# Score groups interleaved with value products in attention, and a quantiser whose transposes are issued one tile later

## What is computed

```python
def bitlinear(x, W, b):
    w_scale = jnp.clip(jnp.mean(jnp.abs(W)), EPS, None)
    Wq = _ste(W, jnp.clip(jnp.round(W / w_scale), -1.0, 1.0) * w_scale)
    x_scale = jnp.clip(jnp.max(jnp.abs(x), axis=-1, keepdims=True), EPS, None)
    xq = _ste(x, jnp.clip(jnp.round(x * (QB / x_scale)), -QB - 1.0, QB) * (x_scale / QB))
    return jnp.einsum('bnd,hd->bnh', xq, Wq) + b
...
q, k, v = (proj(Wq), proj(Wk), proj(Wv))
attn = jax.nn.softmax(jnp.einsum('bhqd,bhkd->bhqk', q, k) * SCALE, axis=-1)
out = jnp.einsum('bhqk,bhkd->bhqd', attn, v)
...
x = x + attention(xn) + bitlinear(gelu(bitlinear(xn, W1, b1)), W2, b2)
```

## Time and profile before

| | |
|---|---|
| median of the runs | 11071.7 us (11024.9 and 11118.5) |
| profiled execution | 11095.7 us, span of its slowest core 11094.7 us |
| spans of the cores | 10966.5 to 11008.9 us on die 0, 11058.7 to 11094.7 us on die 1 |
| mean granted TensorE clock | 0.76 on die 0, 0.73 to 0.75 on die 1 |
| busy, core 6 | PE 52%, DVE 28%, ACT 21%, POOL 1% |
| attention core of layer 1 | 5782 to 6812 us, 8584 to 9586 us |
| feed-forward net of layer 1, from the first product | 7055 to 8307 us, 9829 to 11095 us |

### The profile page before, as it was taken

One profiled execution on the slowest core, in us unless ns is written; L12 is line 12 of the kernel. 1 busy time (PEld: TensorE's weight loads), 2 busy tenths in 40 slices (PEclk: granted clock), 3 DMA queues, 4 the chain that ended last, 5 costly groups with the idle time before them and its releaser, 6 DMA issues.

```text
span 11094.7 us, 92223 instructions; the slowest of 8 cores (10966.5 to 11094.7 us)
## 1 busy us (share of the span) xinstructions
PE 5763.6 (52%) x33686; PEld 3472.2 (31%) x33686; DVE 3077.8 (28%) x4361; ACT 2320.9 (21%) x2412; POOL 131.9 (1%) x197
## 2 busy tenths in 40 slices
PE   0111124455785454468668884255445888425544
PEld 0010012232453232235435553122222555312222
DVE  3423422222101222210122124522233222452223
ACT  0000010000112100011115552211221555321212
POOL 1000000000000000000000000000000000000000
PEclk9999996666796666678867676677677777667776
DMA  7463511221232212223200000022110000002221
GB/s 185 146 137 118 153 60 61 68 69 62 87 121 82 74 61 69 68 78 115 89 23 5 5 5 8 28 79 80 67 61 25 5 5 5 8 27 80 80 68 61
DMA packets 366364, 728.17 MB, mean 66 GB/s; under 512 B 126438, under 2 KB 126695, under 8 KB 361832
## 3 DMA queue, kind: packets, MB, share of 16 engines
q1 hardware_dynamic: 310088, 525.13, 14.8%
q0 software_dynamic: 55840, 197.15, 6.1%
HBM read 663.48 MB, written 77.59 MB: 67 GB/s over the span
## 4 chain that ended last, share of the span: by engine, by line
PE 42%; DMA 21%; DVE 18%; ACT 9%; issue 6%; ACTq 2%; DVEq 1%; SPq 1%; POOLq 0%; POOL 0%
PE pot L1696 7%; PE p1h L1332 4%; PE ph L1033 4%; PE pss L1654 4%; ACT c1At L1658 4%; DMA wna<-L_ffn_W 3%; PE pob L1062 3%; PE pq L778 3%; DMA wnb<-L_ffn_W 3%; PE p1o L1448 3%; DMA f1wf<-s_w2t 2%; PE pk L820 2%; PE pk L822 2%; DMA gwall<-s_L_attn_WqB 1%; DMA gwall<-s_L_attn_WvB 1%
## 5 line engine op out<-in xcount | busy, mean ns | idle before, releaser
L1658 ACT ACTIVATE c1At<-pss,shift_col 128x1024 bf16<-128x1024 f32 x1024 | 1077.0, 1112 | 688.7 <-PE pss L1654 685.0
L1654 PE MATMUL pss<-c1qch,a1kfm 64*128 64x256 bf16 x4096 | 701.9, 311 | 324.7 <-ACT c1At L1658 309.7
L1696 PE MATMUL pot<-c1At,a1vtok 128*65 128x256 bf16 x4096 | 825.7, 387 | 0.0
L1696 PEld LDWEIGHTS pot<-c1At,a1vtok 128*65 128x65 bf16 x4096 | 636.7, 162 | 180.8 <-issue 80.9
L1392 PE MATMUL p1u<-ident_bf,f1q2s 128*128 128x128 bf16 x1024 | 129.6, 302 | 942.5 <-ACT f1q2s L1379 918.5
L1332 PE MATMUL p1h<-xqfm,f1wf 128*128 128x512 bf16 x2048 | 499.1, 389 | 117.3 <-DMA f1wf<-s_w1t 112.1
L1654 PEld LDWEIGHTS pss<-c1qch,a1kfm 64*128 64x128 bf16 x4096 | 370.4, 103 | 583.6 <-issue 495.0
L820 PE MATMUL pk<-gwall,xnfm 128*128 128x512 bf16 x768 | 354.0, 461 | 361.3 <-DMA gwall<-s_L_attn_WvB 172.9
L1033 PE MATMUL ph<-xnfm,f0w 128*128 128x512 bf16 x2048 | 511.9, 415 | 48.7 <-DMA f0w<-s_w1t 35.1
L1062 PE MATMUL pob<-f0stash,f0w 128*128 128x256 bf16 x4096 | 494.3, 286 | 40.0 <-DMA f0w<-s_w2t 29.4
L1448 PE MATMUL p1o<-f1wf,f1ght 128*128 128x512 bf16 x2048 | 473.7, 388 | 47.9 <-DMA f1wf<-s_w2t 37.4
(11 more groups left out here) (217 smaller groups left out, 7455.2 us busy)
## 6 DMA issues: line engine op xcount, KB each, us to landing
wna<-L_ffn_W SPq DMA_DIRECT2D x128, 512.0 KB, 5.3
wnb<-L_ffn_W SPq DMA_DIRECT2D x32, 2048.0 KB, 12.1
f0w<-s_w1t SPq DMA_DIRECT2D x128, 512.0 KB, 3.6
f0w<-s_w2t SPq DMA_DIRECT2D x128, 512.0 KB, 3.7
f1wf<-s_w1t SPq DMA_DIRECT2D x128, 512.0 KB, 3.6
f1wf<-s_w2t SPq DMA_DIRECT2D x128, 512.0 KB, 3.7
gwall<-s_L_attn_WqB POOLq DMA_DIRECT2D x16, 2048.0 KB, 9.7
gwall<-s_L_attn_WkB POOLq DMA_DIRECT2D x16, 2048.0 KB, 9.7
```

Of the source, the lines that this page charges most:

```text
L1654: mm = b.pe.matmul(psp[k][:, kt4 * QCH:(kt4 + 1) * QCH], kf, qf, start=True, stop=True)
L1658: se_done[k] = b.tick(b.se.activation(Ath[:, kg * 4 * QCH:(kg + 1) * 4 * QCH], psp[k][:], AF.Exp, bias=st.shift_col[:], scale=0.125), "se")
L1696: mm = b.pe.matmul(potp[h % 2][:], va, Ath[:, kt * QCH:(kt + 1) * QCH], start=(kt == 0), stop=(kt == NKT - 1))
```

## The change

In the attention core, `emit_scores(h)` becomes `emit_scores_grp(h, kg)`, which emits one of the four groups. The first head's groups are emitted together as before. In the loop, groups 0 and 1 of head h+1 come ahead of the value products of head h, group 2 comes behind the eighth of the 16, and group 3 behind the sixteenth, ahead of `emit_ot` of head h-1. In the feed-forward net, the body of the quantiser is cut into three functions: `emit_red` (reductions and small steps), `emit_sr` (scaling and rounding) and `emit_trq` (transposes and copies back). Tile t runs `emit_red(t)`, then `emit_trq(t-1)`, then `emit_sr(t)`; the transposes of the last tile follow behind the loop. The statistics have two tiles in turn, and ACT waits for a given count of PE, that of the transposes of the tile before (for the first tile those of the block before), where it waited for PE's whole count.

```diff
-    qst = A("qst", [P, 4], F32)
+    qst2 = [A(f"qst{i}", [P, 4], F32) for i in (0, 1)]
...
-        for tt in range(4):
+        def emit_red(tt):
             gt_sl = ght[:, tt * FF:(tt + 1) * FF]
+            qst = qst2[tt % 2]
             b.ve.drain()
             b.wait(b.ve, "se")
             b.ve.reduce_max(qst[:, 0:1], gt_sl[:, 0:2048], axis=AX.X,
...
             b.tick(b.ve.drain(), "ve")
+
+        def emit_sr(tt, tr_gate):
+            gt_sl = ght[:, tt * FF:(tt + 1) * FF]
+            qst = qst2[tt % 2]
+            qv = 0
             for hh in range(2):
                 hsl = slice(hh * 2048, (hh + 1) * 2048)
                 b.wait(b.se, "ve")
-                b.wait(b.se, "pe")
+                if tr_gate:
+                    b.se.wait_ge(b.sem["pe"], tr_gate)
...
+            return qv
+
+        def emit_trq(tt, qv):
             with (nc.psum_tensor(_psname(st, "p1u"), [P, 512], BF16) as pu0,
                   nc.psum_tensor(_psname(st, "p1u"), [P, 512], BF16) as pu1):
                 pup = [pu0, pu1]
                 b.wait(b.pe, "se", qv)
...
+            return pv
+
+        qpend = None
+        for tt in range(4):
+            emit_red(tt)
+            if qpend is not None:
+                tr_gate = emit_trq(*qpend)
+            else:
+                tr_gate = prev_trq
+            qv = emit_sr(tt, tr_gate)
+            qpend = (tt, qv)
+        prev_trq = emit_trq(*qpend)
...
-            def emit_scores(h):
+            def emit_scores_grp(h, kg):
...
-            emit_scores(0)
+            NG = NKT // 4
+            for kg in range(NG):
+                emit_scores_grp(0, kg)
             pend = None
             for h in range(H):
                 if h + 1 < H:
-                    emit_scores(h + 1)
+                    for kg in range(min(2, NG)):
+                        emit_scores_grp(h + 1, kg)
                 b.pe.wait_ge(b.sem["se"], exps_of[h])
...
                     mm = b.pe.matmul(potp[h % 2][:], va,
                                      Ath[:, kt * QCH:(kt + 1) * QCH],
                                      start=(kt == 0), stop=(kt == NKT - 1))
+                    if kt == 7 and h + 1 < H and NG > 2:
+                        emit_scores_grp(h + 1, 2)
                 pv = b.tick(mm, "pe")
+                if h + 1 < H and NG > 3:
+                    emit_scores_grp(h + 1, 3)
                 if pend is not None:
                     emit_ot(*pend)
                 pend = (h, pv)
```

More of the change, by code:

```diff
@@ L1285, in _ffn1 @@
     prevo = {}
+    prev_trq = 0
     for ob in range(S // 512):
@@ L1378, in _ffn1 @@
                 b.wait(b.se, "ve")
-                qv = b.tick(b.se.activation(q2s[:, hsl], scf[:], AF.Identity,
+                qv = b.tick(b.se.activation(q2s[:, hh * 2048:(hh + 1) * 2048],
+                                            scf[:], AF.Identity,
                                             scale=qst[:, 2:3]), "se")
+            return qv
+        def emit_trq(tt, qv):
             with (nc.psum_tensor(_psname(st, "p1u"), [P, 512], BF16) as pu0,
@@ L1385, in _ffn1 @@
                 ev = {}
+                pv = 0
                 for jb in range(FT_ // 4):
@@ L1645, in emit_scores @@
                 Ath = At2[h % 2]
[L1646 to L1660, removed]
+                k = kg % 2
+                if k in se_done:
+                    b.pe.wait_ge(b.sem["se"], se_done[k])
+                for kt4 in range(4):
+                    kt = kg * 4 + kt4
+                    kf = kfm[(h % 2) * 64:(h % 2) * 64 + 64,
+                             (h // 2) * S + kt * P:(h // 2) * S + (kt + 1) * P]
+                    mm = b.pe.matmul(psp[k][:, kt4 * QCH:(kt4 + 1) * QCH],
+                                     kf, qf, start=True, stop=True)
+                pv = b.tick(mm, "pe")
+                b.wait(b.se, "pe", pv)
+                se_done[k] = b.tick(b.se.activation(
+                    Ath[:, kg * 4 * QCH:(kg + 1) * 4 * QCH], psp[k][:],
+                    AF.Exp, bias=st.shift_col[:], scale=0.125), "se")
                 exps_of[h] = se_done[k]
```

## The result

| | before | after |
|---|---|---|
| median | 11056.99 us (10 runs, 10947.62 to 11118.49) | 10734.1 us (11 runs, 10509.87 to 10886.75) |
| ratio, after to before | | 0.9592 [0.9494, 0.969] |
| profiled execution, span | 11094.7 us | 10552.6 us |
| granted TensorE clock over the span, by core | 0.732 to 0.764 | 0.787 to 0.802 |

A forecast was written before the change was run, and what follows sets the result against it. Bound: an attention chain alternating between PE and ACT, whose gaps also lower PE's clock. From the profiled 11095.7 us, less 406 (attention) and 20 (quantiser), 10670; median forecast 10645 us, range 10520 to 10780.

The forecast's parts named there:

- The head: Attention loop, one head: 7.25 us in the old trace; forecast 4.85 at 2.4 GHz, 5.58 at 0.81, 5.14 on the mean.
- The term for changes between score and value products: PE in the attention loop: four switches between the product kinds a head at 0.07 us, 0.28 together.
- the share of the middle level: Attention on the slowest cores: 40% of heads taken at granted clock 0.81, bounds none and all.
- The chunk: Attention, 256 queries with 16 heads: 98.7 us against 124.1, so 406 us less over 16 chunks.
- The first head behind the thin start: Start of each attention chunk, where score groups still wait for one another: one head at the lower clock, 7.8 us.
- The gap: From the last head's first value product to the next chunk's: 21.2 us less two exponentials, 19.2.
- The quantiser: Second feed-forward layer: only first transposes go under the reduction; 11.7 us between tiles becomes 10.85, 20 us less in all.
- rival (2): Attention: granted clock at the middle level everywhere, heads 5.58 us, chunk 104.3, kernel 10735 us; chance 0.20.
- (1): The forecast itself, 10645 us; 10580 with no heads at clock 0.81, 10680 with six in ten; chance 0.60.
- (3): Attention: the clock swing survives, half of each head at 0.50, heads 6.3 us, kernel 10885 us; chance 0.10.
- (4): Attention gains nothing: PE's product changes stall it some 2 us a head; only the quantiser's gain remains, 11050 us; chance 0.06.
- (5): Slower: one gap a head holds the clock at 1.2 GHz through the chunk, 141.1 us, kernel 11325 us; chance 0.04.

The follow-up runs named there:

- e3: Kernel before, old order, with eleven unread score products a head placed in PE's two gaps: 10711 us median against 11063.75.
- e9: Kernel before, old order, with eleven unread value products a head ahead of the 16, on the path that sets the head: 11131.9 us median against 11036.9.
- e12: Kernel before, old order, with four unread score products a head in PE's gaps (3 and 1): 10932.6 us in one run, against 11036.87.
- e11: Changed kernel with group 2's four score products split into two pairs, behind the sixth and tenth value product: 11097.7 us; kernel before 11036.87.
- e5: Kernel before with only the attention half of the change, quantiser as before: 10777.7 us (four runs) against 11001.9.
- e6: Kernel before with only the quantiser half of the change, attention as before: 11074.9 us (one run) against 11001.9.
- e7: Changed kernel with quantiser waits naming the needed counts, and copies and reductions placed on DVE while ACT works: 10364.2 us, ratio 0.9353 to before.
- e10: Changed kernel with twelve of the 16 value products a head left out, so the output is wrong: 10670.7 us (three runs); kernel before 11036.87.

## Why the prediction was right, and where its sizes were off

**What bounds the kernel: right.** A chain that alternates between PE and ACT, with the clock following its gaps. e3, e9 and e12 show the second half, in which the argument was thinnest: with the gaps filled and the order left alone the clock is at 1.00 in the steady heads (0.94 over the attention) and the value products take half the time.

**The head: right in form, two terms off.** The chain is the one written down: from group 3's first product to group 1's it is 1.96 us in the trace as in the sum (6005.61 to 6007.57). The profile shows 0.65 us of them as idle where the prediction, which counted from starts, had near 1. The term for changes between score and value products was 0.07 each; it measured 0.11 (6003.08 to 6004.08 is eight products, 0.87, and 0.13; from there to 6004.62 four, 0.44, and 0.10; e11's two extra changes cost 0.22). So the head at the upper level is 5.01 us, not 4.85; just over the upper bound of 5.0. The other way went the share of the middle level, 40% of heads: in the profiled execution the cores' attention shows 1.00 and 0.50 alone. Together 5.01 us where 5.14 was forecast: two errors of opposite sign, so part of the nearness is luck. The Trainium skill ("TensorE: Matmul & The Clock Gate", Part 1, the warning on the peak-current limiter) would have had every head at 13/16; 195 of the 240 intervals between core 5's heads at 5.01 us and a window at 1.00 don't agree for this execution. Nor is the level held over the stage in e5's, where core 2 has 0.81 over 5950 to 5969 us and 1.00 over 6070 to 6110.

**The chunk: right.** Forecast 98.7 us, measured 96.5. The first head behind the thin start was put at 7.8 and took 6.75 to 7.98; in four chunks it was three or four heads and not one. The last head was 4.5 and took 4.6. The gap was 19.2 and took 17.8 to 18.2 but for two of near 19.5, as in PE's timeline of after:

```profile
5766.49 1.91 PE L1723 MATMUL pot<-c1At,a1vtok 128*65 128x256 bf16 x16 [1.29 <-ACT c1At L1682]
...
5770.36 7.15 PE L1642 MATMUL pq<-xnfm,a1wall 128*128 128x256 bf16 x64 [0.58 <-DVE c1otok L1704]
...
5784.28 1.07 PE L1723 MATMUL pot<-c1At,a1vtok 128*65 128x256 bf16 x4
```

Its 64 projection products take 7.15 us where the earlier trace rows had 7.88: the granted clock is 1.00 over them, where a window over those of the earlier trace rows reads 0.89. The prediction took the gap's products at their old price.

**The quantiser: right.** 11.7 us between ACT's last activation of a tile and its next one should become 10.85: it is 11.0 (7118.79 to 7129.79), and the row names the copy L1410 as what it waits for, as the prediction read from the waits. 0.74 x 24 = 18 us against 20. e6 shows it alone, e7 what the wait and the places together cost.

**The sum.** Forecast for the profiled execution 10670 us, measured 10553.6, 116 less. Attention gave some 440 and not 406; the quantiser's 18 of 20 are lost in FF stages that were 11 us longer on the slowest core; and 115 us, as much as the whole miss, lie ahead of layer 1's attention, where no line changed. There core 6 of before was granted 0.81 for 1038 us of the first 5600 and core 5 of after for none. This is scatter that the sum has no term for. The median, 10734 for a forecast of 10645, lies in the range, but 181 us over the profiled execution where the prediction allowed 50 either way for the scatter; its terms don't contain that. That the median lies 89 us from the forecast is therefore in part luck: its errors go both ways. That it nearly equals rival (2)'s 10735 proves nothing: the heads of 5.58 us are not in the trace of after.

**The rivals.** (1) is what happened. (2) and (3): not in the attention of the profiled execution of after, but both in e5's, which has the same attention. On its core 2, 21 heads take 5.64 us at 0.81, where (2) had 5.58; 67 take 6.88, swinging as (3) has it, but between 0.81 and 0.50, where (3) had 6.3. No rival joined the two, and by e5 the dearer one is the more frequent there. Only one execution of after has a trace, so how often such heads come in it is open. (4), a stall of some 2 us at changes of product: 4 x 0.11 = 0.44. (5), slower because one gap a head holds the clock at 1.2 GHz, was given 0.04, on the ground that the clock rose after a stretch at 0.50 in which PE was shown busy throughout. That ground was weak. In e11 PE is shown busy 78.31 of 80 us at 0.50 and nothing rises; 8.23 us a head there and 5.42 in e10 are this rival. The Trainium skill ("Trainium Kernel Development and Optimization", Performance Expectations) calls the matmul busy time a bad metric for how close a kernel is to roofline, because matmuls are pipelined. e11 agrees that it says little here: PE is shown busy 97.9% of the window at 0.50, where 32 products at 0.214 us make 6.85 of a head's 8.23, and 89% of a window at 0.91. Forecasting faster was right, but with two changes of product more a head the whole gain is gone (e11), and no row that the prediction shows tells the two apart. That the clock stayed up in after was in part luck.

## What to carry to other kernels

When PE shares a loop with another engine and the trace shows its products at two durations, price the loop at both clocks, and try unread products in the gaps first: that takes one small edit and says how much of the loop is the clock's (here four fifths of 201 us a sequence). Taking work or gaps out of such a loop isn't safe by count alone: e11 was slower than after with equal work, and e10's attention with less. A reordering that leaves a wait on an engine's whole count gets little (18 us here); naming the counts that are needed, with the work placed in the gaps that this opens, gave 286.

## What the runs showed of the hardware

- Unread products made the kernel faster: eleven a head in PE's gaps, 10711 us against 11064.
- Leaving out three quarters of the value products made the attention slower, 814 to 824 us a sequence against 792 to 803, with nearly every head at a granted clock of 0.50 (e10).
- The same loop has steady heads of 5.01 us at a granted clock of 1.00; where the upper level is 0.81 it takes 5.64, or swings between 0.81 and 0.50 at 6.88 (e5, core 2).
- The same instructions have two steady paces, 5.23 and 8.23 us a head in e11, and stay at the slower one for long stretches.
- A change between score products (64-row weights) and value products (128-row weights, 65 columns) costs PE about 0.11 us beyond the product (5.01 us a head with four, 5.23 with six). Which of the differences between the two costs it no run shows.
